# Second attention with three float32r products for the weighing, its Pool and image buffers rearranged, and layer norms that carry additions, loads and clears

## The reference

```python
x = x + jnp.tanh(g_xattn[0]) * _L0_xattn_ref(_layernorm(x, axis=-1), ctx_768, ctx_768, ...)
x = x + jnp.tanh(g_ffn[0]) * _L0_ffn_ref(_layernorm(x, axis=-1), ...)
x = x + jnp.tanh(g_xattn[1]) * _L1_xattn_ref(_layernorm(x, axis=-1), ctx_768, ...)
...
```

```python
q = (x @ Wq).reshape(B, Nq, h, dh)
k = (context @ Wk).reshape(B, Nk, h, dh)
v = (context @ Wv).reshape(B, Nk, h, dh)
scores = jnp.einsum('bqhd,bkhd->bhqk', q, k) * scale
attn = jax.nn.softmax(scores, axis=-1)
out = jnp.einsum('bhqk,bkhd->bqhd', attn, v).reshape(B, Nq, h * dh)
return out @ Wo + bo
```

## Time and profile before

| | |
|---|---|
| median of three runs | 4717.48 us (4715.63 to 4719.13) |
| profiled execution, own time | 4710.85 us |
| its span | 4709.2 us |
| mean granted TensorE clock | 0.89 of full speed |
| PE busy | 3802.0 us, 81% |
| DVE busy | 2832.7 us, 60% |
| ACT busy | 2051.6 us, 44% |
| POOL busy | 1444.2 us, 31% |

### The profile page before, as it was taken

How to read it: one execution, slowest core, us unless ns; L and a number is a source line. 1 busy time by engine, 2 the same in 40 slices (tenths; PEclk the granted TensorE clock), 3 DMA queues, 4 the chain that set the end, 5 groups by cost and what they waited for, 6 DMA issues and landing times. The chain is left out here.

```text
span 4709.2 us, 86688 instructions
## 1 busy us (share of the span) xinstructions
PE 3802.0 (81%) x32862; PEld 2475.0 (53%) x32862; DVE 2832.7 (60%) x3540; ACT 2051.6 (44%) x2875; POOL 1444.2 (31%) x1905
## 2 busy tenths in 40 slices
PE   7389889952557999997999996499585888888875
PEld 7156556631334666664666663277332555555553
DVE  8566555643335555534555543477546999989982
ACT  7166666630112434332343442266222666656651
POOL 0265344303213223212332310022005555545510
PEclk9689999976867999997999997799796999989996
DMA  6166666633413323312332320111004665556620
GB/s 165 44 149 151 136 140 146 149 104 134 149 24 90 87 79 85 80 47 62 87 87 79 86 61 15 41 44 31 17 0 100 138 137 129 133 124 138 138 71 14
DMA packets 197062, 434.60 MB, mean 92 GB/s; under 512 B 45708, under 2 KB 98878, under 8 KB 196589
## 3 DMA queue, kind: packets, MB, share of 16 engines
q1 hardware_dynamic: 122196, 338.87, 28.7%
q0 software_dynamic: 38912, 47.06, 4.7%
q10 hardware_dynamic: 35616, 43.97, 3.5%
HBM read 244.72 MB, written 32.67 MB: 59 GB/s over the span
## 5 line engine op out<-in xcount | busy, mean ns | idle before, releaser
L1401 DVE TENSOR_REDUCE L_mp<-ps 112x2 f32<-112x1000 f32 x384 | 458.2, 1198 | 549.4 <-PE ps L1223 545.9
L1260 PE MATMUL ps<-L_p,L_cn 125*97 125x448 f32 x1536 | 639.2, 538 | 0.0
L1384 ACT ACTIVATE L_p<-ps 125x896 f32<-125x896 f32 x384 | 352.2, 917 | 634.5 <-PE ps L1248 562.1
L2064 DVE TENSOR_REDUCE L_mp<-ps 112x2 f32<-112x1000 f32 x384 | 456.4, 1193 | 72.1 <-PE ps L1865 57.0
L2030 ACT ACTIVATE L_p<-L_p 125x896 f32<-125x896 f32 x384 | 364.8, 950 | 258.1 <-DVE L_p L2081 257.1
L885 ACT ACTIVATE L_p<-ps,rk 125x896 f32<-125x896 f32 x384 | 385.8, 1005 | 164.3 <-PE ps L763 144.9
L2081 DVE SCALAR_TENSOR_TENSOR L_p<-ps,xn 125x896 f32<-125x896 f32 x384 | 414.9, 1081 | 28.9 <-DMA xn<-L_low 20.2
L1246 PE MATMUL ps<-L_qh,L_ch 97*125 97x448 f32 x768 | 385.7, 502 | 14.2 <-DMA L_qh<-L_mc 14.2
L1260 PEld LDWEIGHTS ps<-L_p,L_cn 125*97 125x97 f32 x1536 | 250.4, 163 | 205.8 <-issue 165.9
L1897 PE MATMUL ps<-L_p,L_vs 125*18 125x112 f32 x6144 | 233.5, 272 | 120.2 <-ACT L_p L2030 104.5
L1223 PE MATMUL ps<-L_cr,L_qb 96*112 96x500 f32 x768 | 271.6, 440 | 37.8 <-DMA L_cr<-in_ctxT 32.6
(11 more groups left out here) (518 smaller groups left out, 7185.8 us busy)
## 6 DMA issues: line engine op xcount, KB each, us to landing
L_ks<-L_k_part SPq DMA_DIRECT2D x288, 375.0 KB, 9.7
L_ks<-L_k_first SPq DMA_DIRECT2D x96, 375.0 KB, 7.1
moe_w<-in_L_w SPq DMA_DIRECT2D x64, 512.0 KB
L_cn<-in_ctxN SPq DMA_DIRECT2D x32, 568.4 KB
cs_ct<-in_ctxT SPq DMA_DIRECT2D x32, 562.5 KB
L_raw<-in_ctxT SPq DMA_DIRECT2D x32, 562.5 KB
L_cr<-in_ctxT POOLq DMA_DIRECT2D x32, 562.5 KB, 4.8
L_ch<-in_ctxT POOLq DMA_DIRECT2D x32, 562.5 KB
```

The lines of the kernel that those rows point to most:

```text
L1260: mm = nc.tensor.matmul(U[:, a, :], CN[s][:, j, :], P[:, n % 2, a * HALF:(a + 1) * HALF], start=(j == 0), stop=(j == KT - 1))
L1384: nc.scalar.activation(two(P[:, n % 2, :]), SB[n % 2], ACT.Exp).then_inc(S["exped"].sem, 1)
L1401: nc.vector.tensor_reduce(mp[:, 2 * k:2 * k + 2], ps[0:TT, bank:bank + 2, 0:500], AX.X, ALU.max).then_inc(S["chunk_maxed"].sem, 1)
L2064: nc.vector.tensor_reduce(mp[:, 2 * c:2 * c + 2], ps[0:TT, CB[pair], 0:500], AX.X, ALU.max).then_inc(S["chunk_maxed"], 1)
```

## The change

In the second attention W(k) becomes three float32r products for each half, like S(k). `P` is split into PH (exp written as float32r by ACT, a second exp before the one for `P`) and PL (the rest, one DVE subtraction of two SBUF inputs, 125x896, named `split`). The rows are split into CNH (a casting POOL transfer, `first_rows`) and CNL (a POOL subtraction of 125x1164, `rest_of_rows`). Raw keys and raw rows now share one SBUF buffer, RAW, for both batches, and SP loads each when POOL is done with the last. The image pieces lie in `xn`; so M and `xn` are stored to DRAM during the first half's `make_queries` and loaded back at the start of the second's. At the start of a half POOL does the first-pass inputs first. Layer norms can carry the gated addition by column quarters, the loads of the block after them, the clearing of old semaphores (`new_signals(True)`) and, in the last feed-forward, the binarizing of the weights.

```diff
 def attend_wide
-    CN = [sb(f"cn{s}", [KP, KT, KA]) for s in range(2)]
+    CNH = [sb(f"cnh{s}", [KP, KT, KA], F32R) for s in range(2)]
+    CNL = [sb(f"cnl{s}", [KP, KT, KA], F32R) for s in range(2)]
     P = sb("p", [KP, 2, HQ])
-    RAW = [sb(f"raw{s}", [DC, NK]) for s in range(2)]
+    PH = sb("ph", [KP, 2, HQ], F32R)
+    PL = sb("pl", [KP, 2, HQ], F32R)
+    RAW = sb("raw", [KP, NK])
...
# SP, body
-                        sp.wait_ge(*at(f"keys_split{s}", 3 * i + 3))
+                        sp.wait_ge(*at(f"rows_split{1 - s}", i + 1 + s))
                         raw_keys(i + 1, s)
-                        sp.wait_ge(*at("weighed", 24 * i + 12 * s + 14))
+                        sp.wait_ge(*at(f"keys_split{s}", 3 * i + 5))
                         rows(i + 1, s)
...
# Pool
+            def first_rows(i, s):
+                pool.dma_start(flat(CNH[s][:, :, :]), batch(d["ctxN"], i, s)).then_inc(S[f"rows_hi_in{s}"].sem, 16)
+            def rest_of_rows(i, s):
+                pool.wait_ge(*at(f"rows_in{s}", 16 * i + 16))
+                pool.wait_ge(*at(f"rows_hi_in{s}", 16 * i + 16))
+                nc.gpsimd.tensor_tensor(flat(CNL[s][:, :, :]), raw_rows, flat(CNH[s][:, :, :]).bitcast(F32),
+                                        ALU.subtract).then_inc(S[f"rows_split{s}"].sem, 1)
...
# PE, weigh
-                pe.wait_ge(*at("exped", 24 * i + n + 3))
+                pe.wait_ge(*at("p_split", 24 * i + n + 1))
                 for a in range(2):
-                    mm = nc.tensor.matmul(U[:, a, :], CN[s][:, j, :], P[:, n % 2, a * HALF:(a + 1) * HALF],
-                                          start=(j == 0), stop=(j == KT - 1))
+                    q = slice(a * HALF, (a + 1) * HALF)
+                    nc.tensor.matmul(U[:, a, :], CNH[s][:, j, :], PH[:, n % 2, q], start=(j == 0), stop=False)
+                    nc.tensor.matmul(U[:, a, :], CNH[s][:, j, :], PL[:, n % 2, q], start=False, stop=False)
+                    mm = nc.tensor.matmul(U[:, a, :], CNL[s][:, j, :], PH[:, n % 2, q], start=False,
+                                          stop=(j == KT - 1))
# PE, body
                         chunks(i + 1, k // 12, k % 12)
-                    if k % KT:
-                        weigh(i, k)
-                        aside(i, k, prev, nxt)
-                        make_image(i, k, nxt)
                     if k + 2 < 24:
                         score(i, k + 2)
                     elif nxt:
                         score(i + 1, k - 22)
-                    if k % KT == 0:
-                        aside(i, k, prev, nxt)
-                        weigh(i, k)
+                    weigh(i, k)
+                    aside(i, k, prev, nxt)
+                    make_image(i, k, nxt)
# ACT, body
+                    nc.scalar.activation(two(PH[:, n % 2, :]), SB[n % 2], ACT.Exp)
                     nc.scalar.activation(two(P[:, n % 2, :]), SB[n % 2], ACT.Exp
                                          ).then_inc(S["exped"].sem, 1)
# DVE
+            def split(i, n):
+                dve.wait_ge(*at("exped", 24 * i + n + 3))
+                nc.vector.tensor_tensor(PL[:, n % 2, :], P[:, n % 2, :], PH[:, n % 2, :].bitcast(F32),
+                                        ALU.subtract).then_inc(S["p_split"].sem, 1)
                         chunk_max(i + 1, k // 12, k % 12)
+                    if k + 1 < 24:
+                        split(i, k + 1)
+                    elif nxt:
+                        split(i + 1, 0)
 def make_queries
+            if half == 0:
+                sp.dma_start(kept[0], flat).then_inc(moved.sem, 16)
+                sp.dma_start(kept[1], src[:, :]).then_inc(moved.sem, 16)
+                sp.wait_ge(moved.sem, 32)
+            else:
+                sp.dma_start(flat, kept[0]).then_inc(moved.sem, 16)
+                sp.dma_start(src[:, :], kept[1]).then_inc(moved.sem, 16)
...
+            if half:
+                pe.wait_ge(moved.sem, 64)
```

More of the change, by code:

```diff
@@ L70, in __init__ @@
         self.eps = self.sb("eps", [128, 1])
-        self.signals, self.part = [], 0
+        self.signals, self.done, self.part = [], [], 0
         self.new_signals()
@@ L81, in sig, with new_signals @@
         return s
-    def new_signals(self):
+    def new_signals(self, later=False):
         nc, old = self.nc, self.signals
-        if old:
+        if later:
+            self.done += old
+        elif old:
             with nc.Block() as block:
@@ L190, in _ @@
                     loads(sp)
+            if done:
+                @block.gpsimd
+                def _(pool):
+                    nc.clear_and_free_semaphores([s.sem for s in done])
             @block.tensor
@@ L217, in _, with add @@
                 link = core.linker(dve, "dve")
+                def add(c):
+                    tile, gate = gated
+                    nc.vector.scalar_tensor_tensor(out=core.xT[:, columns(c)], in0=tile[:, columns(c)],
+                                                   scalar=core.tg[:, gate:gate + 1], in1=core.xT[:, columns(c)],
+                                                   op0=ALU.mult, op1=ALU.add).then_inc(added.sem, 1)
+                if gated:
+                    add(0)
                 for c in range(NCH):
+                    if gated and c + 1 < NCH:
+                        add(c + 1)
                     dve.wait_ge(mean.sem, mean.at(c + 1))
@@ L229, in _ @@
                     finish(link)
-        for s, n in ((mean, NCH), (cen, NCH), (sq, NCH), (var, 1), (std, 1), (inv, 1), (spread, NCH)):
+                if aside:
+                    aside.vector_last(dve, link)
+        for s, n in ((added, NCH if gated else 0), (mean, NCH), (cen, NCH), (sq, NCH), (var, 1), (std, 1), (inv, 1), (spread, NCH)):
             s.base += n
[L234 to L243, removed]
 CS = 4
@@ L416, in fold_weights, with load @@
         nw = 16 * len(loads)
-        with nc.Block() as block:
[L418 to L422, removed]
+        def load(sp):
+            for dst, name in loads:
+                sp.dma_start(dst, d[f"{L}_{name}"]).then_inc(w_in.sem, 16)
+            sp.wait_ge(w_in.sem, nw)
+        if norm:
+            norm(load)
+        with nc.Block() as block:
+            if not norm:
+                block.sync(load)
             if N is None and not keep_max:
@@ L1029, in attention_wide @@
                 qp = core.sb(f"{L}_qp{half}", [DC + 8, HB, HQ], F32, ctx)
-                make_queries(core, qp, M, cq, src, scale, half)
+                with ExitStack() as c1:
+                    M = core.sb(f"{L}_M{half}", [D, H, KA], F32, c1)
+                    if half == 0:
+                        fold_weights(core, L, M, N, cq, scale, True, 64, None, norm)
+                    make_queries(core, qp, M, cq, src, scale, half, kept)
                 attend_wide(core, f"{L}{half}", S, qp, N, bo, half, ctx, bit, image)
@@ L1137, in body @@
                         invert(i, 0)
-            for s in range(2):
-                raw_keys(0, s)
-                rows(0, s)
+            raw_keys(0, 0)
+            sp.wait_ge(*at("keys_split0", 2))
+            rows(0, 0)
+            sp.wait_ge(*at("rows_split0", 1))
+            raw_keys(0, 1)
+            sp.wait_ge(*at("keys_split1", 2))
+            rows(0, 1)
             pairs(sp, body)
@@ L1330, in load_image @@
             def load_image(i, c):
-                act.dma_start(IX[:, :], image_part(image.first, i, c)).then_inc(S["img_in"].sem, 16)
+                act.dma_start(IX, image_part(image.first, i, c)).then_inc(S["img_in"].sem, 16)
             def value(i, c, again=True):
@@ L1450, in _ @@
             round_image(0, 0, False)
+            split(0, 0)
             pairs(dve, body)
@@ L2878, in quantize_weights, with load @@
         w_in, summed, spread = (core.sig(f"bitw_{n}") for n in ("in", "summed", "spread"))
+        def load(sp):
+            for n in BW:
+                sp.dma_start(w[n][:, :, :], d[f"bit_{n}"]).then_inc(w_in.sem, 16)
+        if norm:
+            norm(load)
         with nc.Block() as block:
-            @block.sync
-            def _(sp):
-                for n in BW:
-                    sp.dma_start(w[n][:, :, :], d[f"bit_{n}"]).then_inc(w_in.sem, 16)
+            if not norm:
+                block.sync(load)
             @block.tensor
@@ L3379, in _, with bit_attention @@
                                          bias=bias).then_inc(S["copied"], 1)
-def bit_attention(core, bit, image):
+def bit_attention(core, bit, image, norm):
     nc, ps = core.nc, core.ps
```

152 lines of the change are left out of this document (86 added, 66 removed).

## The result

| | before | after |
|---|---|---|
| median | 4716.56 us (4 runs) | 4796.11 us (4 runs, 4783.41 to 4800.69) |
| span of the profiled execution | 4709.2 us | 4797.8 us |

The changed kernel takes 1.0166 times as long, interval 1.0143 to 1.0188: 79.6 us more. The prediction said 4756 us with a range from 4658 to 4805. Direction and range held; of the size it had half, and the forecast's own range, 4725 to 4790, was missed by 6 us.

What follows compares the result with a forecast made beforehand. PE alone was taken to bound the pairs. Image waits less W's gain +19, last pairs -10, lock +81, outside the pairs -51: +39 on 4717.5 gives 4756 us, range 4658 to 4805.

Steps and rivals of the forecast that it cites:

- W at S's price: In each step, W's six float32r products cost 1.23 us as in S, not 1.48: 6.0 us less a pair.
- The image's hole: After an image matmul the next C waits for ACT's copy of bank 7: PE idles 1.05 us, six times a pair.
- The projection: At k = 10 its copy must be out before C(11): a wait priced like the image's, 1.05 us.
- The lock: In the pairs, POOL's SBUF work stops DVE's split: 5.8 us a pair, +81; rival without it (0.26): 4675 us.
- the sign that had been named: In the profile after, the split's mean above 1.09 us and some over 3 us, ending where a POOL subtraction ends.
- k = 23: Step 23 of a pair: negation waits for CL, QL goes next, the split ends at 7.95; PE idles 3.4 us.
- k = 5 to 7: UN and CNL back to back: the first split slips in before, the second waits for CNL, 1.3 us.
- the clock: Rival: the clock falls to 1.2 GHz in the 3.4 us hole at k = 0, +40 to +80; chance 0.12.
- Outside the pairs: Starts of halves, reload, weights under norms, gated additions, clears and last feed-forward together: -51 us.
- The starts: At the start of each half, first S comes at 38.4 us instead of 51.6: -13 a half, -26.
- the reload: The second half loads M and xn back before its queries: +10 us.
- the pairs' term: Second attention's pairs: +19 for image waits less W's gain, -10 for each half's last pair, +81 for the lock.

Runs made afterwards that it cites:

- outside_head: The changed kernel with the second attention's pairs as in the kernel before, keeping only the changes outside the pairs: 4659.3 us, 0.9891 of the kernel before.
- ahead_light: The changed kernel with the image matmul ahead of W and DVE's two image reductions cut to 8 of 500 columns: 4734.5 us, 1.0060.
- pool_light: The changed kernel with POOL's subtractions CL, QL and CNL cut to 32 columns from the second pair on: 4689.5 us, 0.9952.

## Why the prediction was right, and where its size was off

- **W at S's price: right.** Rows after stand 0.20 to 0.21 apart (1711.31, 1711.52, 1711.72 above).
- **The image's hole: right in place and size.** 84 times 1.12 us by starts, 94 in all, where 1.05 had been forecast. The projection, priced alike, was too dear: its wait shows 3.7 us in six pairs of a half, 0.6 each. The two errors cancel: 94 and 8 against the 103 of the forecast.
- **The lock: right as a mechanism, and shown.** By POOL's work taken away 107 us come back, by the split taken away 133; with only one of the two in the kernel, PE waits 5 us and none for the split. The split's mean is 1.33 us and its longest 4.88 (line 1502 in the profile after), the sign that had been named; it ends 0.95 behind a POOL instruction and not with it. The Trainium skill's rule (SBUF — State Buffer, "SBUF: two separate sides"), that the pair is held for the whole instruction, is what the trace after shows at CL: a negation of 0.17 us takes 2.40.
- **Its price: 57 us and not 81 as waits for the split, in other places than said.** At k = 23 I let QL go before the split and priced 3.4; in the trace the split goes first, 1.03. At k = 5 to 7 I wrote that the first split slips in before UN, and priced 1.3; UN starts 0.95 before it, CNL follows without a turn for DVE, and PE idles 1.88.
- **Not in the sum: a late DVE makes its maxima late too.** I had costed the maximum at nothing, since DVE's 2.3 of 2.9 us would catch up in the image's holes. PE waited 34 us for it.
- **Not in the sum but among the rivals: the clock.** It was to fall in the hole at k = 0; 12 of its 18 falls came at or behind the hole at k = 5 to 7, and all 18 cost 38 us, just under the 40 to 80 named. Its chance had been 0.12. The forecast and this rival came true together, which the list, with one or the other, did not provide for.
- **Outside the pairs: right.** The starts gave 27 (13 and 14 by the offsets of the same instruction between the traces; 26 said), the reload cost 6 (10 said), the weights under the norm gave 12 (11), the norms, additions, clears and the last feed-forward 26 (24). -59 against -51, and outside_head measured it alone: 4659.3 where 4717 - 58 = 4659 had been worked out.

The step that was mis-sized is thus the pairs' term: +19 - 10 + 81 = +90 forecast. By the lengths the pairs brought 1429 - 1282 = +147. Of the 57 more the maxima are 34 and the falls of the clock 38, less the 24 by which the splits cost below their price; the 9 that are left lie in waits too short for the table and in long products outside the falls. Per pair and in the first half that is -6.0 for W, +7.7 for the copies, +3.4 for the splits, +2.1 for the maxima and +1.8 in falls, 9.0 of the measured 9.7, and in the second, with 3.5, 2.6 and 3.5 for the last three, 11.3 of 12.0. That the number still lies in the range is in part luck: the splits' smaller price hid a third of what the sum had left out.

What stays open: why POOL passes DVE by between UN and CNL and not in the other 34 meetings, and why DVE's maxima are still late in ahead_light.

## What to carry to other kernels

When a change brings the second engine near the first (here DVE is busy for 77 us of a pair and PE for 80), price its lateness as a whole, not wait by wait: the holes that it catches up in are then part of its schedule, and closing them wins little until the load is gone (25 us with the split, 74 without it). Where two engines exclude each other, look for two instructions back to back on the one that nobody waits for; one wait that pulls them apart gave 54 us. And test the parts of a large change alone: here the parts beside the headline were worth 56 us (59 by the traces) and the three products with their new order cost 137 (4796.1 - 4659.3).

## What the runs showed of the hardware beyond the forecast

- **Who is next where POOL and DVE exclude each other.** Where POOL went from CL to QL (18 times), from QL to QB (14) or from CNL to QB (2) and a negation or a split of DVE was waiting, DVE had the next turn each time, in all 34 such meetings of the trace after. (One negation that began 0.05 us before the end of a QL, at 2370.64, was held through the QB behind it.) Where UN was followed by CNL, POOL went on, 14 times of 14, and the split ended 3.6 us after UN.
- **Holes of under 2 us were often followed by 3.4 to 13.7 us of the lower clock.** In the trace after the granted clock falls 18 times inside the pairs, 11 times for 3.4 us, 6 times for 6.8 and once for 13.7. Each fall lies at or just behind a hole of PE of 1.48 to 2.76 us, or two of 0.78 to 1.00 us whose ends are 1.4 us apart. Three holes of 1.59 to 1.65 us had no fall behind them. The many single 1.0 us holes of the image's copy let it fall nowhere in pool_light.
